# Two loops over an expert's further tiles on TensorE: empty rounds put first, and a test around the loop of single tiles

## What is computed

```python
def _L0_ffn_ref(x, gate_w, gate_b, w1, b1, w2, b2):
    flat = x.reshape(-1, D)
    logits = flat @ gate_w + gate_b
    topv, topi = lax.top_k(logits, TOP_K)
    topw = jax.nn.softmax(topv.astype(jnp.float32), axis=-1).astype(x.dtype)
    routing = jnp.zeros_like(logits).at[jnp.arange(T)[:, None], topi].set(topw)
    def body(acc, params):
        W1e, b1e, W2e, b2e, we = params
        h = jax.nn.gelu(flat @ W1e + b1e, approximate=False)
        out = h @ W2e + b2e
        return (acc + out * we[:, None], None)
    final, _ = lax.scan(body, init, (w1, b1, w2, b2, routing.T))
x = x + _layernorm(_L0_attn_ref(_layernorm(x), ...))
x = x + _layernorm(_L0_ffn_ref(_layernorm(x), ...))
```

## Time and profile before

| | us |
|---|---|
| median of three runs | 684.59 |
| lowest and highest run | 682.51, 687.83 |
| profiled execution, its span | 684.8 |
| TensorE busy with matmuls in it | 561.2 |
| VectorE busy | 426.6 |
| ScalarE busy | 366.6 |

### The profile page before, as it was taken

One profiled execution on the slowest core, in us unless ns is written; L12 is line 12 of the kernel. 1 busy time (PEld: TensorE's weight loads), 2 busy tenths in 40 slices (PEclk: granted clock), 3 DMA queues, 4 the chain that ended last, 5 costly groups with the idle time before them and its releaser, 6 DMA issues.

```text
span 684.8 us, 14985 instructions
## 1 busy us (share of the span) xinstructions
PE 561.2 (82%) x4170; PEld 507.0 (74%) x4175; DVE 426.6 (62%) x1446; ACT 366.6 (54%) x820; POOL 185.8 (27%) x153
## 2 busy tenths in 40 slices
PE   2768756766855789999999999999999899999930
PEld 1636344344345588999999999989989899999930
DVE  4858856936885675645455545658657855545467
ACT  3364732734733535463646466567668646363571
POOL 2000071071072166231314131311312323231320
PEclk9968977967987989999999999999999999999975
DMA  8910020091021176332323235356356323232459
GB/s 215 382 50 0 1 101 23 0 327 58 1 101 40 51 196 214 55 46 46 46 47 46 47 46 156 56 135 188 54 153 169 47 48 46 46 46 46 108 154 306
DMA packets 51850, 66.75 MB, mean 97 GB/s; under 512 B 4870, under 2 KB 45292, under 8 KB 51692
## 3 DMA queue, kind: packets, MB, share of 16 engines
q1 hardware_dynamic: 37804, 47.87, 22.3%
q0 software_dynamic: 14016, 18.56, 15.7%
HBM read 38.26 MB, written 28.74 MB: 98 GB/s over the span
## 4 chain that ended last, share of the span: by engine, by line
PE 59%; DVE 9%; issue 9%; ACT 8%; another core or an unknown queue 6%; DMA 6%; DVEq 1%; POOLq 0%; ACTq 0%; POOL 0%; SPq 0%
PE pY L1546 25%; PE pL L1534 22%; DMA sum_y<-y,dest 4%; PE pP L722 3%; PE pP L823 2%; PE pS L739 2%; ACT xn L569 2%; PE pX L439 2%; ACT xrow L636 1%; PE pT L707 1%; ACT h L624 1%; DMA w_stage<-sum_y 1%; ACT probs L602 1%; PE pT L817 1%
## 5 line engine op out<-in xcount | busy, mean ns | idle before, releaser
L1469 ACT ACTIVATE h<-pL,b_now 128x256 f32<-128x256 f32 x272 | 112.3, 464 | 154.0 <-PE pL L1534 146.5
L517 POOL DMA_INDIRECT sum_y<-y,dest x70 | 114.2, 1631 | 284.8 <-DVE y L1590 271.9
L1546 PE MATMUL pY<-w_hi,h_lo 128*128 128x256 f32 x544 | 154.2, 284 | 4.4 <-DVE h_lo L1563 4.1
L1534 PE MATMUL pL<-xeT_hi,w_lo 128*128 128x256 f32 x544 | 151.7, 279 | 6.4 <-issue 5.6
L1563 DVE TENSOR_TENSOR h_lo<-h,h_hi 128x512 fp32r<-128x512 f32 x136 | 93.0, 691 | 94.4 <-ACT h_hi L1475 88.3
L1546 PE MATMUL pY<-w_hi,h_hi 128*128 128x256 f32 x544 | 151.3, 278 | 0.5 <-issue 0.4
L1546 PE MATMUL pY<-w_lo,h_hi 128*128 128x256 f32 x544 | 151.0, 278 | 0.5 <-issue 0.5
L1534 PE MATMUL pL<-xeT_lo,w_hi 128*128 128x256 f32 x544 | 151.1, 278 | 0.0
L1534 PE MATMUL pL<-xeT_hi,w_hi 128*128 128x256 f32 x544 | 150.9, 277 | 0.0
L1534 PEld LDWEIGHTS pL<-xeT_hi,w_lo 128*128 128x128 f32 x544 | 102.0, 188 | 7.7 <-issue 6.9
L1546 PEld LDWEIGHTS pY<-w_hi,h_lo 128*128 128x128 f32 x544 | 102.2, 188 | 6.6 <-DVE h_lo L1563 5.6
(11 more groups left out here) (266 smaller groups left out, 844.0 us busy)
## 6 DMA issues: line engine op xcount, KB each, us to landing
w_stage<-w SPq DMA_DIRECT2D x16, 1024.0 KB
xt<-sorted_x SPq DMA_DIRECT2D x38, 260.0 KB
sum_y<-fill SPq DMA_DIRECT2D x1, 4352.0 KB, 19.6
w_stage<-sum_y SPq DMA_DIRECT2D x8, 512.0 KB, 7.6
out<-z SPq DMA_DIRECT2D x8, 512.0 KB, 6.9
x_all<-x SPq DMA_DIRECT2D x3, 1024.0 KB, 8.4
sorted_x<-fill SPq DMA_DIRECT2D x8, 260.0 KB
sum_y<-y,dest POOLq DMA_INDIRECT x70
```

The lines of the kernel that those rows point to most:

```text
L517: pool.indirect_dma_start(out=sum_y, out_offset=bass.IndirectOffsetOnAxis(ap=to[:, i:i + 1], axis=0), in_=rows[:, i, :], in_offset=None, c ...
L1469: a = act.activation(h[:, c, :], pL[:, bk, i * TM:(i + 1) * TM], ACT.Gelu, bias=b1_now[par][:, c:c + 1])
L1534: mm = pe.matmul(pL[:, bk, i * TM:(i + 1) * TM], w[:, 0, col], x[:, k, :], start=(k == 0 and w is lo), stop=(k == KC - 1 and x is xeT_lo))
L1546: mm = pe.matmul(pY[:, i, 0:D], s[:, c, rows], w[:, 1, c * D:(c + 1) * D], start=(c == 0 and s is h_lo), stop=(c == FC - 1 and w is lo))
```

## The change

Both loops keep their three rounds, but the tests are turned round so that the empty rounds come first: a round of four runs if `fours + 4 * u >= TPE - 4`, with TPE = 16, and a round of one if `singles + v >= 3`. The number of the tile is then counted from the end, modulo 64. Around the loop of single tiles stands a new test that passes over the whole loop where `singles` is zero. Only TensorE uses this form of `rest`.

```diff
             def rest(e, who, par, n, base):
                 if roomy:
                     fours = (n + 31) & 28
+                    singles = (n + 3) & 3
                     with eng.If(n >= 5):
                         with eng.Fori(0, TPE // 4 - 1) as u:
-                            with eng.If(fours > 4 * u):
+                            with eng.If(fours + 4 * u >= TPE - 4):
                                 with eng.Fori(0, 4) as v:
-                                    tile(e, who, par, base + 1 + 4 * u + v)
-                    singles = base + 1 + fours
-                    with eng.Fori(0, 3) as v:
-                        with eng.If(((n + 3) & 3) > v):
-                            tile(e, who, par, singles + v)
+                                    tile(e, who, par, (base + fours + 4 * u + v + 65 - (TPE - 4)) & 63)
+                    with eng.If(singles >= 1):
+                        with eng.Fori(0, 3) as v:
+                            with eng.If(singles + v >= 3):
+                                tile(e, who, par, (base + fours + singles + v + 62) & 63)
                     return
```

## The result

| | us |
|---|---|
| kernel before, median of six runs | 684.65 (682.51 to 687.83) |
| changed kernel, median of six runs | 689.36 (688.37 to 694.59) |
| ratio, with its 95% interval | 1.0077 (1.0050 to 1.0104) |
| profiled execution of the changed kernel, time and span | 688.61 and 686.8 |

The change costs 0.77%, 4.7 us by the medians, 3.4 to 7.1 by the interval. The forecast was 687.1, 2.5 us over the runs shown, within 1% and on the slow side. The time lies in the range, but the increase is nearly twice the one forecast.

The account below looks back on a forecast made before the run. TensorE was taken to bound the kernel over the 34 expert tiles, with 5.6 us of waits for its sequencer addressable. Entry terms sum to +2.6 us on a 684.8 span, 687.4; forecast median 687.1, range 683.5 to 690.5.

Parts of the forecast that it names:

- That no round disappears, and the guard never skips: TensorE's tile loops: empty rounds only move ahead of full ones; the test around the singles only costs, 0.34 us.
- The cover of 2.0 us behind a tile: TensorE's sequencer works ahead, so 2.0 us of branches behind a tile are free; anything longer stalls the array.
- Entry 0's end: Behind entry 0's last single the 1.57 us stall and its 0.31 go, but VectorE is late: 0.4 us gained.
- the new wait for h_lo in entry 1's first tile: Sign in the profile after: the second layer waits for h_lo in five places, no longer four, the new one here.
- Entries 1 and 3, no gain at the end: Behind their last singles the issue waits, 0.9 us each, go, but the next tile waits for VectorE: nothing gained.
- Entry 9 hidden: Ahead of entry 9's single a 1.1 us stall plus 0.3, hidden because VectorE waits for row additions: cost 0.
- Entry 1: Behind entry 1's first tile the branches reach 2.5 us: a stall of 0.5 plus 0.3, sum +0.8 us.
- instruction loading: TensorE jumping over bodies not yet executed: bounds 0 and 1 to 1.5 us once, in entry 1; taken as 0.
- rival B: Slower for good: every jump over or back at the single body meets unheld code, +12 us, about 699; chance 0.03.
- The sum: Entries 0, 1, 3 and 7 give +1.1 + 0.8 + 0.6 + 0.1 = +2.6 us, entry 9 nothing.
- entry 7, up to entry 9: New stall of 1.15 us behind entry 7's first tile, the 1.09 before its singles goes: sum +0.1 us.
- rival C: Stalls in entries 7 and 0 each followed by five slow layers, +2 us, plus 1.5 code load: 690.6; chance 0.15.

Follow-up runs that it names:

- guard_only: Kernel before plus only the test around the single rounds, rounds in the old order: 683.12 us against 682.02, ratio 1.0005.
- fours_only: Kernel before with only the rounds of four reversed, single rounds as before, no guard: 683.04 us, ratio 0.9988.
- one_loop: All further tiles of an entry in one loop of n - 1 rounds, against the kernel before: 679.00 us against 682.02, ratio 0.9959.
- singles_only: Kernel before with only the single rounds reversed, rounds of four as before, no guard: 690.65 us, ratio 1.0107.
- slot_before: Kernel before, its walk over the entries placed at slot 196 of a block of 256 instructions: 685.99 us against 682.02, ratio 1.0043.
- pad_before: Kernel before with 217 never-executed TensorE instructions ahead of the walk, passed over once: 687.87 us, ratio 1.0046 to the kernel before.
- pad_after: Changed kernel with 217 never-executed TensorE instructions ahead of the walk, passed over once: 694.24 us, ratio 1.0144 to the kernel before.
- slot212_after: Changed kernel, its walk placed at slot 212 of a block: ratio 1.0082 to the kernel before, on the chip with 649.39 us.
- slot_after: Changed kernel, its walk over the entries placed at slot 196 of a block of 256 instructions: 690.19 us, ratio 1.0100 to the kernel before.
- slot222_before: Kernel before, its walk placed at slot 222 of a block: ratio 1.0019 to the kernel before, on the chip with 649.39 us.

## Why the prediction was right in kind and half in size

**That no round disappears, and the guard never skips.** Right. L1313 runs fifteen times in the changed kernel, as L1312 did, and `guard_only` is 1.0005.

**The cover of 2.0 us behind a tile.** Right, and the carrying step. Counted from start to start, less the 0.11 us to the next matmul, the new stalls are 1.10, 0.35 (entry 3), 1.23 and 1.06 us; the forecast had 1.16, 0.3, 1.15 and 1.1. In `fours_only` the part of the change that only trades one stall for another of the same size came out at no difference.

**Entry 0's end: only 0.4 of 1.9 us comes through.** Right in kind. VectorE's branches and low pieces set the start of the second layer. `one_loop` shows it in the row above: with the 1.41 us of waiting for issue gone, 1.24 us of waiting for h_lo stand in entry 1's first tile. The changed kernel shows it too: the new wait for h_lo in entry 1's first tile is there as forecast, 1.01 us at 424.00. That the total stays at four places and not five has another reason: the wait of 0.80 us in the second tile of the walk (274.56 in the kernel before) is missing, because in this execution TensorE waited 2.66 us for the transfer of that tile's rows at 271.02. `fours_only` has such a wait as well (1.24 us), so it isn't of the change.

**Entries 1 and 3, no gain at the end.** Right. The two waits for issue behind their last tiles (0.91 and 0.87 us) are gone, and the waits for h_lo in the next tile grew by 0.82 and 0.85.

**Entry 9 hidden.** Right: VectorE waited 2.33 us in the same place.

**Entry 1.** Here the step failed that priced instruction loading. The text gave its bounds as 0 and 1 to 1.5 us and took 0, "because every taken branch of L1312 took 214 to 216 ns". Those branches jumped over a body that had run; the new ones jump over bodies that had not, and whether such a jump is long the rows could not say: in entry 0 it took 207 ns, in entry 1 2530, and the stall there is 2.86 us and not 0.5. Even the upper bound was too low: I read 1.0 us from the time of a packet, and the branch lasts from 0.2 us before the packet to 1.4 us after it. `singles_only` has the same branch (2952 ns); `fours_only` and `guard_only` have none over 363 and show no cost.
The Trainium skill ("Runtime: NRT & Kernel Launch", "Instruction fetch mechanics") says that a taken branch to a target outside the present two-page window waits for a DMA fetch. The trace agrees for one jump, at 2.5 us. It does not bear out rival B, in which each such jump pays: no kernel has more than one long branch, and no q8 packet comes after 434 us though the loops jump back.

**The sum.** Adding 2.3 us for the branch to the sum of 2.6 gives 4.9, beside 4.7 measured. The two profiles, compared from one place of the walk to the same place of the other, bear the first terms out and not the last:

| stretch, from start to start in the kernel before and the changed one | forecast | measured |
|---|---|---|
| entry 0's single and entry 1's first tile to its second layer (398.12 to 422.68; 398.24 to 424.00) | +1.1 | +1.2 |
| from there to the second layer behind entry 1 (459.03; 463.75) | +0.8, with the branch +3.1 | +3.4 |
| from there to the second layer behind entry 3 (507.54; 512.87) | +0.6 | +0.6 |
| from there to entry 7 (539.46; 543.18) | 0 | -1.6 |
| entry 7, up to entry 9 (539.46 to 634.05; 543.18 to 636.92) | +0.1 | -0.9 |

In the fourth row a wait for h_lo is 2.27 us in the kernel before (533.89) and 0.73 in the changed one (537.62); in `fours_only`, `guard_only`, `slot_before` and `pad_before`, all with the single rounds in the old order, it is 0.6 to 1.1, and over all kernels 0.3 to 2.3, so the 1.6 us are not shown to be of the change. In the fifth, slow layers are missing, as told under rival C. So the profiled pair moves apart by 2.75 us before entry 9, and that 4.9 lies so near the 4.7 of the medians is in part luck.

**A price that the sum left out: the clock.** The text priced the layer behind a stall at 0.31 us more. Behind the wait for issue in entry 1 (2.45 to 3.25 us) the granted clock fell to 0.50 in four of the five kernels that have the single rounds reversed: `singles_only`, `pad_after` and `slot212_after` for 3.4 us each, with a first layer of 7.3 to 7.45 us, and `slot_after` for 6.8. Beside the 5.92 of the changed kernel this is 1.5 us and 2.6. In the changed kernel's profiled execution, whose wait is 2.70, it did not fall there, but it did for 3.4 us behind the 2.66 us wait for rows at 271. From entry 0's single on it fell behind no other wait in any kernel, neither behind those for issue of 1.5 us or less nor behind those for h_lo of up to 2.3. So one execution of the changed kernel may pay 1.5 us more than another, and whether its median holds that price isn't shown.

**Rival C**, slow layers after the stalls, is not what happened at the new stall in entry 7: the chain of waits of the changed kernel has one layer of 5.71 us behind the stall, then 5.46 and 5.44 again.

```profile
554.68 1.07 issue
555.75 5.71 PE pL L1535 x48
561.46 0.44 PE pX L439 x4
561.90 5.46 PE pY L1547 x48
567.36 5.44 PE pL L1535 x48
```

Behind the 2.7 us in entry 1 two layers of 5.66 and 5.65 us follow the one of 5.92. And in the kernel before, four layers of 5.65 or 5.66 us follow the 5.92 behind entry 7's old stall (597.25), which is 0.8 us that the changed kernel does without. The granted clock is 1.00 in both stretches, so it doesn't explain the two paces; what does stays open. So the 0.3 us per stall is uncertain by some tenths, up to 0.8 in one place.

## What to carry to other kernels

A sequencer that runs ahead of the array gives each tile here a budget of free branches of 2.0 us. The branches that a tile takes anyway need 1.0 to 1.3 of it, so one empty round of 0.8 to 1.0 us nearly fills it and a second one stalls the array. Moving empty rounds pays only towards a place with budget left, so list the sequence at both ends before moving; taking the rounds away (a loop with its count in a register) was the version that gained. A forward jump over code that has not run yet can cost 2.5 us where the same jump later costs 0.2. Others did not (207 to 455 ns), and shifting code alone can move or create a long one, so look for it in the sequencer's longest branch and not in the code. A stall of about 2.5 us or more can cost its own length and 1.5 us again, because the clock fell to half behind most of them; look at the granted clock behind every new stall.

## What the runs showed that was not expected

A placing of the loop at slot 196 of a block slowed the kernel before, otherwise unchanged, by 0.43% (0.15 to 0.71), with one branch of 2515 ns. A long branch was 2.5 us in five kernels (2515 to 2536 ns) and 2952 and 3225 in two. And the same kernel took 649.39 us in one of the sessions against 682 to 685 in the others, so times of different sessions can't be set side by side. The profiles put this difference ahead of the expert tiles: the first of them starts at 218 us in `slot222_before` and at 250 in `slot_before`.
